# Cross-attention and int4 feed-forward kernel: fp16 halves for scores and skip of batches 4 to 31, row maxima by scaled tensor_scalar, row-sum split moved to ScalarE

## What is computed

```python
def xattn(pcd_up, pcd_down, Wq, Wk, Wv, Wskip):
    q, k, v = Wq @ pcd_up, Wk @ pcd_down, Wv @ pcd_down
    attention = softmax(q.T @ k / sqrt(128))            # 1024 x 256 for each batch
    return Wskip @ pcd_up + (attention @ v.T).T

def ffn(x, qweight, scales, zeros, bias):
    return x @ dequantized(qweight, scales, zeros) + bias    # 1024 x 1024 weights

x = x + xattn(layernorm(x), ctx, Wq, Wk, Wv, Wskip)
x = x + ffn(layernorm(x), qweight, scales, zeros, bias)
```

## Time and profile before

| what | value |
|---|---|
| median of 3 runs | 517.6 us (517.2 to 517.63) |
| the profiled execution's own time | 517.71 us |
| span of its trace, first to last instruction | 515.6 us |
| busy share of the span: PE, DVE, ACT, POOL | 96%, 84%, 73%, 91% |
| granted TensorE clock, mean | 1.000 of 2.4 GHz |
| one step in the middle (280.35 to 295.49 us) | 15.14 us |
| busy in that step: PE, DVE, ACT, POOL | 15.14, 13.33, 11.60, 14.50 us |

### The profile page before, as it was taken

How to read it: one execution, slowest core, us unless ns; L and a number is a source line. 1 busy time by engine, 2 the same in 40 slices (tenths; PEclk the granted TensorE clock), 3 DMA queues, 4 the chain that set the end, 5 groups by cost and what they waited for, 6 DMA issues and landing times.

```text
span 515.6 us, 9359 instructions
## 1 busy us (share of the span) xinstructions
PE 496.5 (96%) x2672; PEld 299.4 (58%) x2672; DVE 435.3 (84%) x1001; ACT 376.8 (73%) x867; POOL 467.1 (91%) x711
## 2 busy tenths in 40 slices
PE   4888999999999999999999999999999999999987
PEld 3544456665666656566665566666556666565644
DVE  4989898888988888898888889888889888887752
ACT  4889778777787777778777777877777877777520
POOL 4786999999999999999999999999999999999763
PEclk9999999999999999999999999999999999999999
DMA  8774678778968987887878786787767687757653
GB/s 305 204 156 108 183 176 157 204 187 187 197 171 202 156 199 183 196 182 179 211 150 193 185 206 176 180 204 156 196 178 197 172 202 190 168 130 145 167 130 120
DMA packets 227203, 92.65 MB, mean 180 GB/s; under 512 B 209488, under 2 KB 214352, under 8 KB 227152
## 3 DMA queue, kind: packets, MB, share of 16 engines
q1 hardware_dynamic: 226432, 91.91, 73.9%
q10 hardware_dynamic: 720, 0.14, 0.2%
HBM read 23.87 MB, written 16.78 MB: 79 GB/s over the span
## 4 chain that ended last, share of the span: by engine, by line
PE 83%; POOL 8%; issue 3%; DVE 3%; ACT 2%; DMA 1%; POOLq 0%; ACTq 0%; SPq 0%
PE ps_y L1020 38%; PE ps_e L974 15%; PE ps_o L1015 13%; PE ps_o L1009 7%; PE ps_kv L992 2%; PE ps_y L1026 2%; PE ps_kv L988 2%; POOL sb_prob L273 2%; POOL sb_xn_lo L318 2%; PE ps_e L970 1%; POOL sb_o L267 1%; DMA sb_x<-in_x_dram 1%; ACT sb_prob L506 1%; POOL sb_rstd L281 1%; DVE sb_neg_max L697 1%
## 5 line engine op out<-in xcount | busy, mean ns | idle before, releaser
L1020 PE MATMUL ps_y<-sb_wf,sb_xnt_hi 128*128 128x512 f16 x496 | 188.3, 380 | 3.3 <-DMA sb_xnt_lo<-sb_xn_lo 3.3
L1020 PE MATMUL ps_y<-sb_wf,sb_xnt_lo 128*128 128x512 f16 x496 | 188.0, 379 | 0.0
L506 ACT ACTIVATE sb_prob<-ps_e,sb_neg_max 128x256 f32<-128x256 f32 x256 | 118.2, 470 | 51.5 <-DVE sb_neg_max L697 51.4
L273 POOL TENSOR_SCALAR sb_prob<-sb_prob,sb_rsum 128x256 f32<-128x256 f32 x256 | 122.5, 492 | 7.3 <-DVE sb_rsum L702 7.2
L706 DVE TENSOR_TENSOR sb_p_lo<-sb_prob,sb_p_hi 128x1024 f16<-128x1024 f32 x64 | 78.1, 1220 | 36.5 <-ACT sb_p_hi L515 36.4
L267 POOL TENSOR_TENSOR sb_o<-sb_prod,sb_x 128x512 f32<-128x512 f32 x63 | 84.9, 1348 | 5.8 <-DVE sb_prod L740 5.8
L697 DVE TENSOR_REDUCE sb_neg_max<-ps_e 128x2 f32<-128x512 f32 x128 | 85.0, 682 | 1.8 <-PE ps_e L970 1.4
L515 ACT ACTIVATE sb_p_hi<-sb_prob 128x1024 f16<-128x1024 f32 x64 | 67.4, 1053 | 23.3 <-issue 23.3
L1020 PEld LDWEIGHTS ps_y<-sb_wf,sb_xnt_hi 128*128 128x128 f16 x496 | 48.4, 98 | 61.0 <-DMA sb_xnt_lo<-sb_xn_lo 4.3
L1020 PEld LDWEIGHTS ps_y<-sb_wf,sb_xnt_lo 128*128 128x128 f16 x496 | 48.5, 98 | 54.8
L974 PE MATMUL ps_e<-sb_k_hi,sb_xc_hi 128*128 128x256 f32 x224 | 78.6, 351 | 0.1
...
## 6 DMA issues: line engine op xcount, KB each, us to landing
...
sb_pt_hi<-sb_p_hi SPq DMA_TRANSPOSE x64, 3.0
sb_pt_lo<-sb_p_lo SPq DMA_TRANSPOSE x64, 2.9
...
sb_xnt_hi<-sb_xn_hi SPq DMA_TRANSPOSE x32, 2.8
```

The source lines that it names most:

```text
L273: last = pool.tensor_scalar(prob[:, b % 2, j, t, :], prob[:, b % 2, j, t, :], rsum[:, j, t:t + 1], P_SCALE, ALU.mult, ALU.mult)
L506: done = act.activation(prob[:, b % 2, j, t, :], ps_e[j % 2][:, t, :], ACT.Exp, bias=neg_max[:, j, t:t + 1], accum_out=esum[:, j, t:t + 1])
L1020: pe.matmul(ps_y[h][:, :], xnt_p[s][:, q % 2, kt, :], wf[:, kt, h * HALF:(h + 1) * HALF], start=kt == 0 and s == 0, stop=False)
```

## The change

For batches 4 to 31 the split operands of scores and skip become fp16 instead of fp32r. fp16 has a smaller range, so they are scaled: `centre` now writes the full first layernorm times 1024 (it multiplies by the inverse deviation as well, with `nb1` as bias, the product made by the new `mean_product` on DVE), and the keys, values and skip weights are scaled by factors that `scales_of(n)` works out on DVE in place of `value_scale(n)`. The scores then come out scaled, and each batch has its own factor `e_scale`. So `row_max` no longer reduces a chunk with one tensor_reduce; it multiplies each 128 x 256 tile by the factor with a tensor_scalar and accumulates the minimum, two instructions for a chunk, whose products go to `prob`, where `exps` overwrites them. `exps` has the factor as a scale operand. The row-sum split of batches 2 to 31 moves from POOL to ACT, around `xn_high(a)` and after the next step's `centre`. A few instructions at the start prepare bounds (`constants`, `key_maximum`, `key_bound`, `key_bound_sum`).

```diff
-        xc_hi, xc_lo = (sb(n, [P, 3, N], F32R) for n in ("xc_hi", "xc_lo"))
-        k_hi, k_lo = (sb(n, [P, 2, M], F32R) for n in ("k_hi", "k_lo"))
+        xc_hi, xc_lo = (sb(n, [P, 3, N], F16) for n in ("xc_hi", "xc_lo"))
+        k_hi, k_lo = (sb(n, [P, 2, M], F16) for n in ("k_hi", "k_lo"))
...
-        wsk_hi, wsk_lo = (sb(n, [C, 3, C], F32R) for n in ("wsk_hi", "wsk_lo"))
+        wsk_hi, wsk_lo = (sb(n, [C, 3, C], F16) for n in ("wsk_hi", "wsk_lo"))
...
                 if ran(a):
-                    split_row_sum(a)
                     xn_low(a)
...
-                act.activation(xc[:, :] if n >= WHOLE else x_whole[:, n, :], x_sb[:, n % 4, :],
-                               ACT.Identity, bias=mv1[:, 0:1], scale=-1.0).then_inc(xc_done, 1)
+                act.activation(xc[:, :], x_sb[:, n % 4, :], ACT.Identity, bias=nb1[:, :],
+                               scale=rstd1[:, n % 2:n % 2 + 1]).then_inc(xc_done, 1)
...
                     done = act.activation(prob[:, b % 2, j, t, :], ps_e[j % 2][:, t, :], ACT.Exp,
-                                          bias=neg_max[:, j, t:t + 1], accum_out=esum[:, j, t:t + 1])
+                                          bias=neg_max[:, j, t:t + 1], scale=1.0 if b < WHOLE else e_scale[:, b % 2, 1:2],
+                                          accum_out=esum[:, j, t:t + 1])
...
+            def row_sum_high(a):
+                act.wait_ge(xn_done, a + 1)
+                act.wait_ge(xnt_loaded[(a - 1) % 2], nth(a - 1, 2, 32))
+                act.activation(row_parts[:, 0:3], rs2[:, 0:1].broadcast_to((P, 3)), ACT.Copy).then_inc(rs_part, 1)
+
+            def row_sum_rest(a):
+                act.wait_ge(rs_part, 3 * (a - 2) + 1)
+                act.activation(rs_rest[:, :], row_parts[:, 0:1], ACT.Identity, bias=rs2[:, :],
+                               scale=-1.0).then_inc(rs_part, 1)
...
                 if ran(n):
                     centre(n)
+                if ran(a - 1) and a - 1 >= 2:
+                    row_sum_low(a - 1)
...
                 if ran(a):
+                    row_sum_high(a)
                     xn_high(a)
+                    row_sum_rest(a)
...
+            def mean_product(m):
+                dve.wait_ge(rstd1_done, m + 1)
+                if m > WHOLE:
+                    dve.wait_ge(xc_done, m)
+                dve.tensor_scalar(nb1[:, :], mv1[:, 0:1], rstd1[:, m % 2:m % 2 + 1], -1.0, ALU.mult,
+                                  ALU.mult).then_inc(nb1_done, 1)
...
+            def scales_of(n):
+                dve.wait_ge(kv_done, n + 1)
+                dve.wait_ge(bound_row_done, 1)
+                dve.scalar_tensor_tensor(tops[:, :], ps_m[:, HALF - 1:HALF].broadcast_to((P, 2)), TINY,
+                                         bound_rows[:, :], ALU.max, ALU.mult).then_inc(t_step, 1)
+                dve.wait_ge(t_step, 4 * n + 1)
+                dve.tensor_tensor(tops[:, :], tops[:, :], floors[:, :], ALU.max).then_inc(t_step, 1)
+                dve.wait_ge(t_step, 4 * n + 2)
+                dve.reciprocal(inv_tops[:, :], tops[:, :]).then_inc(t_step, 1)
+                dve.tensor_scalar(o_scale[:, n % 3:n % 3 + 1], tops[:, 0:1], w_inv[:, :], None, ALU.mult)
+                dve.tensor_scalar(e_scale[:, n % 2, :], signs[:, :], tops[:, 1:2], None, ALU.mult).then_inc(t_step, 1)
...
             def row_max(b, j):
                 dve.wait_ge(scores_done[j], b + 1)
-                dve.tensor_reduce(neg_max[:, j, :], ps_e[j % 2][:, :, :], AX.X, ALU.max,
-                                  negate=True).then_inc(max_done[j], 1)
+                if b < WHOLE:
+                    dve.tensor_reduce(neg_max[:, j, :], ps_e[j % 2][:, :, :], AX.X, ALU.max,
+                                      negate=True).then_inc(max_done[j], 1)
+                    return
+                dve.wait_ge(t_step, 4 * (b + 1))
+                for t in range(TPC):
+                    last = dve.tensor_scalar(prob[:, b % 2, j, t, :], ps_e[j % 2][:, t, :], e_scale[:, b % 2, 0:1], None,
+                                             ALU.mult, ALU.min, accum_out=neg_max[:, j, t:t + 1])
+                last.then_inc(max_done[j], 1)
...
                 if ran(n):
-                    value_scale(n)
+                    scales_of(n)
...
+                if ran(m):
+                    mean_product(m)
                 if ran(n):
                     keys_lo(n)
                     values_lo(n)
```

More of the change, by code:

```diff
@@ L320, in xn_low, with constants @@
                 last.then_inc(xnlo_done, 1)
+            def constants():
+                for tile, values in ((floors, (SKIP_TOP / V_TOP, 0.0)), (signs, (1.0 / XN_SCALE, -1.0 / XN_SCALE))):
+                    for k in range(2):
+                        pool.memset(tile[:, k:k + 1], values[k]).then_inc(consts_made, 1)
+                pool.memset(bound_rows[:, 0:1], 1.0 / V_TOP).then_inc(consts_made, 1)
             zp_count = [0]
@@ L527, in apply_norm2, with row_sum_low @@
                                accum_out=rs2[:, :]).then_inc(xn_done, 1)
+            row_parts = xn_lo[:, KT, :].bitcast(BF16)
+            def row_sum_high(a):
[6 more added lines that the diff above has]
+                               scale=-1.0).then_inc(rs_part, 1)
+            def row_sum_low(a):
+                act.wait_ge(rs_part, 3 * (a - 2) + 2)
+                act.activation(row_parts[:, 3:5], rs_rest[:, 0:1].broadcast_to((P, 2)), ACT.Copy).then_inc(rs_part, 1)
+                act.wait_ge(rs_part, 3 * (a - 2) + 3)
+                act.activation(row_parts[:, 5:6], row_parts[:, 3:4], ACT.Identity, bias=rs_rest[:, :],
+                               scale=-1.0).then_inc(rs_done, 1)
             def xn_high(a):
@@ L866, in run_in @@
                 probs_lo(2, 1)
+                mean_product(4)
                 scale_product(0, 0)
@@ L994, in keys_values, with key_bound_sum @@
                 last.then_inc(kv_done, 1)
+            def key_bound_sum():
+                pe.wait_ge(kmax_done, 1)
+                pe.wait_ge(proj_kept, 2)
+                pe.matmul(ps_m[:, HALF - 2:HALF - 1], ones[:, :], kmax[:, :], start=True, stop=True).then_inc(kbound_done, 1)
             def second_keys():
```

76 lines of the change are left out of this document (55 added, 21 removed).

## The result

The change makes the kernel slower: **572.0 us** (median of 4 runs, 571.66 to 572.25) against 517.4 us for the kernel before on the same chip, a ratio of 1.106 with a 95% interval of 1.104 to 1.108. The forecast was 545 us in a range of 519 to 570. The sign was as forecast, and so was the place, DVE's own loop. The size was not: the loss is 54.6 us instead of 27, and the larger part of it comes from two small instructions that the prediction had priced like their short neighbours.

The account below looks back on a forecast made before the run. PE was taken as the bound, with DVE's loop 0.44 us a step behind; -0.44 + 1.16 + 0.27 = +0.99 us a step, +26.7 over 27 steps, ends +0.5, on 517.7 gave 545 us, range 519 to 570.

Parts of the forecast that it names:

- DVE's own loop: DVE's work from `p_lo` to `ve2`, then 4.12 us latency through POOL and ACT; about 14.68 us a step without PE.
- The 0.44 us of room: DVE's waits for PE, 0.11 and 0.33 us a step, by which its loop is shorter than PE's step.
- the small DVE instructions: Five instructions of `scales_of` on DVE, priced at 0.78 us against 0.63 for `value_scale`: +0.15 us a step.
- The row maxima: On DVE, four reductions become eight passes with accumulated minimum, 0.445 us each: +1.16 us a step.
- the one of the free accumulator: Rival on DVE's passes: accumulator written without its own instruction, pass 0.33 to 0.37 us, 520 to 529 us; chance 0.20.
- two elements a cycle: Rival on DVE's passes: they run at double rate, PE stays the bound, 509 to 517 us; chance 0.11.
- a reading that waits: Rival on DVE: accumulator reading waits for the pass, 0.48 to 0.605 us each, 553 to 580 us; chance 0.18.
- `mean_product`: New product on DVE ahead of `ve2`, so on the loop: +0.12 us a step.
- ACT: Row-sum instructions and second operands, at most 2.2 us a step, hidden by ACT's 3.3 us of waits: cost 0.
- POOL's relief: POOL loses four small instructions, `rs_rest` alone averaging 1079 ns; worth 0 in the middle of the kernel.
- The ends: Longer last-step chunks, partly offset by `rs_rest` on POOL, and small instructions at the start: together +0.5 us.
- PE's saving: Cheaper score and skip products on PE, 0.33 us a step; would not show because PE waits for DVE and ACT.

Follow-up runs that it names:

- The constant passes alone: Kernel before with row maxima of batches 4 to 31 as two passes a chunk, constant factor -1 and accumulated minimum: 518.9 us, ratio 1.003.
- the spare instruction: Kernel before plus one unused two-column DVE tensor_scalar with a constant behind the scales of the fifth and later batches: 530.5 us, one run.
- the run with the context's maximum first: Kernel before with fp16 halves, row-sum split on ACT, and DVE's `context_max` moved ahead of the step's first `p_lo`: 519.4 us, ratio 1.005.

## Why the prediction had the loop right and the size wrong

**The loop** was right, and its room nearly. The 0.44 us of room were read from one step, in which DVE's waits for PE are longer than usual; from start to start they average 0.33 over the 27 steps (0.29 ahead of `t_scale`, 0.04 ahead of the first reduction). The constant passes alone (0.35 us, about the room, 1.4 us lost) and the spare instruction (0.90 us, of which 0.47 show in a step of 15.59 against 15.12) show the room from both sides. DVE's wait for `p_hi` stayed at 36.9 us, and the wait for PE's keys went away, as forecast.

**The step that failed** is the one on the small DVE instructions: "three wait each for the one before (0.18, between 155 and 196 ns), two don't (196 less 0.08, 0.12): 0.78, so +0.15". It took the price of one-column instructions for two-column ones and for one with two SBUF inputs. Measured: 1.98 us, so **+1.35** a step. With that in the place of 0.15 the prediction's sum gives 577 us. In one-column form the scales take 0.62 us, and with them the kernel is at 534 us, inside the range. The prediction weighed the accumulator's reading and the mode of the passes and never asked what DVE shares with POOL. The kernel before had it in sight: POOL's `rs_rest`, on one column, averages 1079 ns, because it stands beside DVE's `p_lo`, and so does `nb` with 0.75. In POOL's timeline of the step of the earlier trace rows it ends at 296.12, the `p_lo` that started at 294.84 at 296.07:

```profile
294.87 1.25 POOL L309 TENSOR_TENSOR sb_rs_rest<-sb_rs,sb_xn_lo 128x1 f32<-128x1 f32 x1
```

The prediction used `rs_rest` as a price to be saved and did not ask why one column takes a microsecond.

**The row maxima** were somewhat too dear. Forecast 0.445 us for a pass, +1.16 a step; measured 0.405 (310.75 to 311.56 for two), +0.84. The base of 0.33 was right (0.34 with a constant), the tile's factor costs 0.06 instead of 0.04, and the reading of the accumulator, though an instruction of its own of 82 ns, adds at most 0.01, since it lies beside the next pass. With 0.405 in the prediction's sum, the rest as it stood, the forecast would have been 536 us; the passes were not what broke it. They erred the other way, so that 545 looked nearer to 572 than the working deserved: that is luck. Of the rivals, the one of the free accumulator was right on the reading's cost and wrong on the pass (0.33 to 0.37); two elements a cycle and a reading that waits are out. The Trainium skill's rule on this, page "VectorE: DVE Perf Modes", section "Two Vector instructions with no wait between them", is right that there are two instructions; no run here shows that the second costs time.

**The smaller terms.** `mean_product` +0.11 (forecast +0.12). `wsk_lo` was costed as before and got shorter: from it to the next instruction were 0.49 us in the step of the earlier trace rows (287.56 to 288.05) and are 0.26 (318.62 to 318.88). Before the change it varied with what POOL was doing, from 0.25 to 0.58 us, and averaged 0.43, so that 0.17 are gained on average. ACT was costed at 0 and cost 0.13: the exponentials rose from 470 to 560 ns, so the last of them, and with it the first `p_lo` and the `nb` that waits behind it, come later, and from `ve2` to the last `p_lo` are 4.25 us (304.76 to 309.01) instead of 4.12. POOL's relief was worth nothing, as forecast, and the run of the split alone shows the same (517.0 us).

**The sum again.** Read from one step each, -0.44 + 0.84 + 1.35 + 0.11 - 0.23 + 0.13 = +1.76 us a step. Measured, from the first pass of batch 4 to that of batch 31 after the change:

```profile
71.38 0.47 DVE L784 TENSOR_SCALAR_CACHE_REDUCE sb_prob<-ps_e,sb_e_scale 128x256 f32<-128x256 f32 x1
```

```profile
530.70 0.47 DVE L784 TENSOR_SCALAR_CACHE_REDUCE sb_prob<-ps_e,sb_e_scale 128x256 f32<-128x256 f32 x1
```

(530.70 - 71.38) / 27 = 17.01 us, +1.89 against 15.12. The 0.13 that are missing come from reading the room and `wsk_lo` in one step. Averaged over the same 27 steps of both timelines the terms are -0.33 + 0.83 + 1.33 + 0.11 - 0.17 + 0.13 = +1.90, in the same order. Over 27 steps that is 51 us. The ends cost 2.8 us instead of 0.5: 1.2 ahead of batch 4 (71.38 against 70.15) and 1.6 behind the last batch's first pass.

**PE's saving** was rightly left out of the sum, but for a weaker reason than the runs have. The prediction held that PE's 0.33 us would not show because DVE and ACT set the step. With fp16 halves alone, where by its loop some 9 us were to be had, the kernel lost 35. Without PE to set the pace POOL and DVE run into each other differently, and what they lose there is more than PE gives. The halves also shorten POOL's `xc_lo`, from 1272 to 1156 ns; whether this or PE's products bring `rstd` into second place, and why the runs stay in that phase, was not tried. That the order of arrival makes the wait is shown by the run with the context's maximum first.

No run measured with an interval beats the kernel before by more than about 0.1%. Fp16 halves with the split on ACT and the context's maximum first come nearest of those that change the products (519.4 us).
